# A two-layer convolution and gated feed-forward kernel: the grouped convolution of tiles 6 to 31 as three fp16 products, with its preparation three steps ahead

## The chip, the cores and the metric

The kernel runs on one core of one Trainium2 chip. The metric is the device time of one execution in microseconds (us); the number compared is the median of repeated executions. The engines are PE (TensorE: products, with weight loads shown apart as PEld), DVE (VectorE), ACT (ScalarE), POOL (GpSimd) and SP, which only issues transfers.

## What is computed

The reference, cut to what matters (x is 64 x 64 x 1024; rows are batch times channel):

```python
# layer 0
y   = conv1d(x, weight, pad=4, groups=4, taps=9) + (cond @ c_weight.T)[:, :, None] + fside_bias
x_q = round(y / a_scale).astype(int8)        # a_scale = max|row of y| / 127
w_q = round(weight / w_scale).astype(int8)   # 1024 x 1024
x1  = x + (x_q @ w_q.T * a_scale * w_scale).astype(float16)
# layer 1
x2  = einsum('boi,bih->boh', agg_w, x1) + agg_b      # 64 x 64 matrix per batch
H, z = x2 @ W.T + b, x2 @ A                          # W 1024 x 1024, A 1024 x 32
w   = soft top-2 gate of 8 experts, from H and z at every second row
out = x1 + H + z-delta weighted by the gate          # rank 32
```

## The kernel before

The 4096 rows are 32 tiles of 128 rows (two batches) by 1024. All engines run one program written out by hand, an order for each engine, tied by semaphores. There are three stages: a start (integer weights transposed, small tensors, tiles 0 to 2), a loop `for c in range(3, 32)` that carries layer 0 and the first part of layer 1, and the part behind it, which is nearly all dense product.

**One step c of the loop, on PE:** `conv(c)` (L470), `mix(c - 3)` (x1 times the 64 x 64 matrices, L516), the integer product of tile c - 2 (L532, two halves of eight), cut by three small things: `row_total(c - 3)` (L493), `max_rows(c)` (L539) and `max_back(c)` (L543); then `tokens_out(c - 1)` (transposes, L501) and at odd c `rank_pair(c - 5)` (L569). The convolution works on a layout of x by phases, `x_ph` (128 x 1032 fp32, three buffers), as 16 fp32 products: first 8 for the groups 0 to 3 with 128 rows, then 8 with 64 rows. Each fp32 product shows as two records. Ahead of group 2 it waits for `f_ready`, since groups 2 and 3 use a bank that the integer product of the tile before leaves free only then.

**On DVE:** at even c `rank_out` (L1342, L1343), `conv_bias(c)` (L1283, into `yb`), `row_max(c)` (L1289), `tile_bound` and `tile_scale` (L1319 to L1326, a power of two for x2 of tile c - 3 from its row sums), `layer0(c - 2, 0)` (L1315), `chan_max(c)` (L1294, L1295), `scales(c)` (L1300 to L1306), `layer0(c - 2, 1)`. **On ACT:** `row_sums` (sums of |x1| of a tile, L862), copies of x2 (L879, L882), the integers (L867), `scale_rows` (eight pieces, L889), and W's sums and high halves (L895, L900, L905). **On POOL:** `add_layer0` (x1 = x + f, L1130, two halves), W scaled and its low half (L1135, L1137).

W is used as an fp16 high and low half (`ffn_wT`), and again in the part behind the loop as eight quadrants of sums, prepared in four parts q: `load_t(q)` (SP), `t_scale(q)` (ACT L910), `t_sums(q)` (POOL L1146, four pieces), `t_high(q)` (ACT L921), `t_low(q)` (POOL L1151). Parts q and q + 2 share their stage, so `load_t(2)` waits for the two pieces of `t_low(0)`. Before, `load_t(0)` to `t_low(0)` lie in the last steps of the loop and `t_sums(1)` among the last tiles.

**Behind the loop** PE runs the last mixes and integer products, `dense` (L606) and, between its pieces, the gate: logits (L589), two maxima (L738, L741), then on DVE and ACT a softmax (exponentials on ACT, L1041 and L1043) whose result PE transposes at L746. After it come the pair products (L792) and the rank products (L774). DVE's result `yb` of L1529 is what L746 waits for.

## Time and profile before

| | before |
|---|---|
| median of 3 runs | 651.67 us (650.98 to 651.74) |
| the profiled execution | 651.48 us, of which the span of the trace is 649.7 |
| PE busy | 634.5 us, 98% of the span; 5898 products |
| DVE / ACT / POOL busy | 374.7 / 327.6 / 322.2 us (58 / 50 / 50%) |
| convolution products (L470) | 1024 records, 96.6 us busy, 390 ns mean |
| mean granted clock of PE | 0.995 |
| transfers | 138.37 MB, mean 213 GB/s |

All rows below are of that execution; times in them count from the start of the span, and the rest of its 651.48 us lies outside the span. A bracket at a row's end gives the idle time of the engine ahead of it and what ended it. Of records that follow one another on PE two can be under way at once, so the time that a group takes is read from its start to the start of the next group, not from its length.

### The profile page before, as it was taken

To read this page: it belongs to the slowest core of one execution; us is meant where nothing else is said; L and a number is where in the kernel's file an instruction comes from. 1 tells how busy PE (TensorE), PEld (TensorE's weight loads), DVE (VectorE), ACT (ScalarE), POOL (GpSimd) and SP (SyncE) were. 2 spreads that over 40 slices of the span, in tenths; PEclk is the share of its full clock that TensorE was granted. 3 is DMA by queue.
4 is the path that set the end of the run, shared out by engine and by line. 5 is a ranking of instruction groups with operands and counts; after the bars stand their busy time and mean duration, and the time that the engine had idled before them with its cause. 6 is when DMAs were issued, how large, how long until landed. Compare 5 with 4: busy or idle time off the path is not lost.

```text
span 649.7 us, 14865 instructions
## 1 busy us (share of the span) xinstructions
PE 634.5 (98%) x5898; PEld 336.7 (52%) x5898; DVE 374.7 (58%) x812; ACT 327.6 (50%) x594; POOL 322.2 (50%) x223
## 2 busy tenths in 40 slices
PE   8789999999999999999999999999999999999997
PEld 6545565556555655555554444444444444444443
DVE  5956657665566556667636795745544433444434
ACT  2858898657668766666663335234323223322100
POOL 3012222227778522225475588785766677656400
PEclk9799999999999999999999999999999999999999
DMA  9969877677789798754629114885554444541103
GB/s 311 338 132 368 313 278 294 215 284 257 278 322 338 281 346 289 254 203 148 206 104 333 59 35 152 300 329 194 177 200 139 163 136 157 194 125 71 65 1 129
DMA packets 46705, 138.37 MB, mean 213 GB/s; under 512 B 13180, under 2 KB 13468, under 8 KB 46465
## 3 DMA queue, kind: packets, MB, share of 16 engines
q1 hardware_dynamic: 41886, 120.65, 53.4%
q10 hardware_dynamic: 4752, 16.78, 6.7%
q8 instruction: 47, 0.77, 0.5%
q14 instruction: 20, 0.16, 0.1%
HBM read 89.13 MB, written 48.28 MB: 212 GB/s over the span
## 4 chain that ended last, share of the span: by engine, by line
PE 79%; DVE 1%; issue 0%; ACT 0%; DVEq 0%
PE ps L792 36%; PE ps L532 12%; PE ps L606 9%; PE ps L470 9%; PE ps L516 3%; PE ps L569 3%; PE ps L774 2%; PE ps L501 2%; PE ps L589 1%; PE ps L543 0%; PE ps L539 0%; PE ps L574 0%; DVE unscale L1487 0%; DVE z_lo L1351 0%; DVE ring L1333 0%
## 5 line engine op out<-in xcount | busy, mean ns | idle before, releaser
L1130 POOL TENSOR_TENSOR x<-x_in,f_both 128x512 f32<-128x512 f32 x64 | 74.0, 1157 | 199.0 <-DVE f_both L1315 199.0
L532 PE MATMUL ps<-wqT,yq_both 128*128 128x512 bf16 x512 | 120.5, 379 | 0.8 <-ACT wsc_b L849 0.8
L470 PE MATMUL ps<-x_ph,conv_w 64*64 64x256 f32 (+1 forms) x1024 | 96.6, 390 | 0.0
L889 ACT ACTIVATE yv<-yb,yinv 128x128 f32<-128x128 f32 x256 | 78.0, 390 | 2.3 <-DVE yinv L1306 2.2
L1283 DVE TENSOR_TENSOR yb<-ps,ybias 128x1024 f32<-128x1024 f32 x32 | 39.2, 1224 | 59.5 <-PE ps L470 59.5
L470 PEld LDWEIGHTS ps<-x_ph,conv_w 64*64 64x64 f32 (+1 forms) x1024 | 52.0, 136 | 35.7 <-issue 14.3
L532 PEld LDWEIGHTS ps<-wqT,yq_both 128*128 128x128 bf16 x512 | 45.2, 97 | 48.2 <-issue 0.9
L1166 POOL TENSOR_TENSOR ring<-ring 128x512 f32<-128x512 f32 x52 | 66.0, 1268 | 4.0
L867 ACT ACTIVATE yq_both<-ps 128x1024 bf16<-128x1024 f16 x32 | 32.7, 1022 | 67.2 <-PE ps L501 67.2
L606 PE MATMUL ps<-ffn_wT,ring 128*128 128x512 f16 x288 | 64.6, 379 | 0.0
L927 ACT ACTIVATE ring<-ring,pair_inv 128x1024 f32<-128x1024 f32 x26 | 28.4, 1140 | 54.4 <-DVE x_ph L1583 14.4
L1315 DVE SCALAR_TENSOR_TENSOR f_both<-ps,tok_scale,wsc_b 128x512 f16<-128x512 f32 x64 | 47.8, 748 | 3.6 <-PE ps L532 2.9
L1596 DVE SCALAR_TENSOR_TENSOR x_in<-ps,unscale,x_in 128x512 f32<-128x512 f32 x30 | 22.5, 751 | 43.8 <-PE ps L792 43.8
L606 PEld LDWEIGHTS ps<-ffn_wT,ring 128*128 128x128 f16 x288 | 27.2, 98 | 32.1 <-issue 0.8
L1596 DVE SCALAR_TENSOR_TENSOR wst<-ps,unscale,wst 128x512 f32<-128x512 f32 x28 | 21.0, 750 | 36.0 <-PE ps L792 35.9
L1289 DVE TENSOR_REDUCE rowmax<-yb 128x8 f32<-128x1024 f32 x32 | 39.0, 1220 | 1.0
L516 PEld LDWEIGHTS ps<-mixT,x 64*64 64x64 f32 x2048 | 35.5, 135 | 5.0 <-issue 1.3
L516 PE MATMUL ps<-mixT,x 64*64 64x64 f32 x2048 | 35.6, 218 | 0.0
L1596 DVE SCALAR_TENSOR_TENSOR x<-ps,unscale,x 128x512 f32<-128x512 f32 x21 | 15.8, 751 | 31.5 <-PE ps L792 31.4
L862 ACT ACTIVATE f_both<-x 128x1024 bf16<-128x1024 f32 x32 | 33.4, 1043 | 0.0
L879 ACT ACTIVATE ring<-ps 128x512 f32<-128x512 f32 x52 | 27.8, 585 | 2.6 <-PE ps L516 2.3
L792 PE MATMUL ps<-ffn_wT,x_part 128*128 128x512 f16 x120 | 27.5, 379 | 0.0
(309 smaller groups left out, 1081.9 us busy)
## 6 DMA issues: line engine op xcount, KB each, us to landing
x_ph<-in_x_phases SPq DMA_DIRECT2D x32, 516.0 KB, 6.1
x_in<-in_x SPq DMA_DIRECT2D x32, 512.0 KB, 6.1
x_scratch<-x SPq DMA_DIRECT2D x32, 512.0 KB, 2.9
x_scratch<-ring SPq DMA_DIRECT2D x26, 512.0 KB, 4.3
ring<-x_scratch SPq DMA_DIRECT2D x26, 512.0 KB, 4.4
wst<-in_w_rows SPq DMA_DIRECT2D x12, 512.0 KB, 5.1
x_in<-x_scratch SPq DMA_DIRECT2D x12, 512.0 KB, 4.5
out<-x_in ACTq DMA_DIRECT2D x12, 512.0 KB, 3.4
```

What stands on the lines that cost most here:

```text
L470: return mm(ps_conv[o, g * 2 * MB:(g + 1) * 2 * MB], conv_w[k, g, w.start + o.start:w.start + o.stop], xp[k, g, :, view], start=first, sto ...
L516: last = mm(bank(2 + e)[j * 64:(j + 1) * 64, k * CH:(k + 1) * CH], x1[b, t % 2, l:l + 64], mixT[b, t, b], start=True, stop=True)
L532: last = mm(acc_bank(t, h), yqT[:, t % 2, p, :], wqT[:, p, h * HALF:(h + 1) * HALF], start=p == 0, stop=p == PH - 1)
L606: last = mm(o, x2_cols[:, x2_slot(n), a, k, :], ffn_wT[:, w, k, h * HALF:(h + 1) * HALF], start=k == 0 and i == 0, stop=k == NL - 1 and i ...
L792: last = mm(b, left(a, k), right(w, k), start=fresh and k == 0 and i == 0, stop=k == 3 and i == 2, skip_group_check=True)
L889: last = A(yv[:, s, :], yb[:, t % 2, s, :], ACT.Copy, scale=yinv[:, s:s + 1], bias=MAGIC)
L1130: g.tensor_tensor(x1[:, t % 2, s], x_in[:, t % 3, s], f16[:, s], ALU.add).then_inc(sem("x1_ready"), 1)
L1166: g.tensor_tensor(o, x, y, op).then_inc(sem("s_sum_ready"), 1)
L1283: v.tensor_tensor(yb[:, t % 2, :, :].rearrange("p (b g) m -> p b g m", b=2), ps_conv.rearrange("p (g b m) -> p b g m", g=GRP, b=2), ybias[ ...
L1289: v.tensor_reduce(rowmax[:, :], yb[:, t % 2, :, :], AX.X, ALU.max, apply_absolute_value=True).then_inc(sem("rowmax_ready"), 1)
L1315: v.scalar_tensor_tensor(f16[:, s], acc_bank(t, h), tok_scale[:, t % 4:t % 4 + 1], wsc_b[:, s], ALU.mult, ALU.mult).then_inc(sem("f_ready" ...
L1596: v.scalar_tensor_tensor(buf, src, unscale[:, t:t + 1], buf, ALU.mult, ALU.add).then_inc(sem("pair_folded"), 1)
```

## The change

From tile 6 on (`SPLIT`), the convolution is `split_conv`: x and the weights are each split in an fp16 high and low half, and three products (high-high, low-high, high-low) take the place of one fp32 product: 48 products of 256 columns for a tile. The first six tiles stay as they are. For each such tile x is scaled by a power of two taken from the sum of |x| in its rows, three steps ahead of its use (`LEAD`): ACT `phase_sums(c+3)`, PE `x_total(c+3)`, DVE `phase_bound`, `phase_scale` and `scale_phases(c+3)` (128 x 1032 fp32, L1444), and one step later ACT `phase_high(c+2)` and POOL `phase_low(c+2)` (128 x 1032). `conv_bias` takes the scale back (now with a scalar, L1392).

What is moved for it: the sums of |x1| (`row_sums`) are taken for tiles 0 to 5 only; the bound for x2's scale is made from |x| and the layer's scales in three batches of tiles, in place of one total a step. W's absolute sums go from ACT to DVE (L1469, c = 3 to 10), its scaling from POOL to DVE (`scale_w`, L1474, at c = 13, 15, ..., 27), its sums from ACT to POOL (`w_halves`) and DVE (L1478), one piece of W every second step. `load_phases` runs further ahead, the load for tile 6 ahead of the first load of W. `t_sums(0)`, `t_low(0)` and `t_sums(1)` stand behind the loop, and `load_t(2)` with them.

```diff
-W_ABS, W_BOUND, W_SPLIT, W_SUMS, W_TURN = 3, 11, 13, 19, 27
+W_ABS, W_BOUND, W_SPLIT, W_SUMS, W_TURN = 3, 12, 13, 11, 27
+LEAD = 3
+SPLIT = 3 + LEAD
+BATCHES = ((0, 28), (28, 30), (30, NT))
...
             for c in range(1, NT + 3):
-                if c == NT + 1:
-                    load_t(2)
+                if c >= 3 and c + LEAD + 1 < NT:
+                    load_phases(c + LEAD + 1)
...
+                if c == 2:
+                    load_phases(4)
+                    load_phases(SPLIT)
...
-                if c == W_SPLIT + 9:
+                if c == NT - 2:
                     load_t(0)
                 if c == NT:
                     fetch_x1(0)
                     load_t(1)
+                if c == NT + 2:
+                    load_t(2)
...
+            def split_conv(t):
+                wait(pe, "xl_ready", splits(t))
+                wait(pe, "yb_ready", t)
...
+                parts = ((0, 0), (1, 0), (0, 1))
...
+                for g in range(GRP):
+                    if g == 2:
+                        wait(pe, "f_ready", 2 * t - 4)
+                    for i in range(3):
+                        part(i, g, lo, slice(0, P), slice(P, 2 * P), here, first=g % 2 == 0)
+                        part(i, g, hi, slice(0, P), slice(0, P), there, first=g % 2 == 0)
+                for g in range(2):
+                    for i in range(3):
+                        part(i, g, lo, hi, slice(0, P), there, last=g == 1)
+                        part(i, g + 2, lo, lo, slice(0, P), there, last=g == 1)
+                        part(i, g, hi, lo, slice(P, 2 * P), here, last=g == 1)
+                        last = part(i, g + 2, hi, hi, slice(P, 2 * P), here, last=g == 1)
...
+            def x_total(t):
+                wait(pe, "xsum_ready", splits(t))
+                wait(pe, "yinv_ready", t - LEAD)
+                wait(pe, "x_bound_ready", splits(t - 1))
...
+            def phase_sums(t):
+                act.wait_ge(sem(f"ph_loaded{ph_sem(t)}"), 16 * ph_count(t))
...
+                A(phase_junk, phases(t), ACT.Abs, accum_out=x_sum[:, t:t + 1]).then_inc(sem("xsum_ready"), 1)
...
+            def phase_high(t):
...
+                A(x_split[:, (t - SPLIT) % 2, 0, :], phases(t), ACT.Copy).then_inc(sem("xh_ready"), 1)
...
+            def scale_phases(t):
+                dve.wait_ge(sem("x_scale_ready"), 2 * splits(t))
+                v.tensor_scalar(phases(t), phases(t), x_up[:, t:t + 1], None, ALU.mult).then_inc(sem("xs_ready"), 1)
...
                 layer0(c - 2, 0)
                 chan_max(c)
+                if SPLIT <= c + LEAD < NT:
+                    phase_scale(c + LEAD)
...
                 layer0(c - 2, 1)
                 low(c - 3, 1)
+                if SPLIT <= c + LEAD < NT:
+                    scale_phases(c + LEAD)
...
+                if 0 <= c - W_ABS < NL:
+                    w_abs(c - W_ABS)
+                if c in split_steps:
+                    scale_w(split_steps.index(c))
+                if c - 1 in sum_steps:
+                    w_sums(sum_steps.index(c - 1))
+                if c == 4:
+                    split_weights()
```

The order on DVE, from the second half of `layer0` in step c = 13 to the row maxima of step 14. Before:

```order
L1315 SCALAR_TENSOR_TENSOR f_both<-ps,tok_scale,wsc_b 128x512
L1342 TENSOR_TENSOR z_lo<-ps,zT 40x256
L1343 TENSOR_TENSOR zT<-ps,z_lo 40x256
L1283 TENSOR_TENSOR yb<-ps,ybias 128x1024
L1289 TENSOR_REDUCE rowmax<-yb 128x8
```

And now:

```order
L1430 SCALAR_TENSOR_TENSOR f_all<-ps,tok_scale,wsc_b 128x512
L1444 TENSOR_SCALAR x_ph<-x_ph,x_up 128x1032
L1474 TENSOR_SCALAR wst<-wst,w_up 128x1024
L1495 TENSOR_TENSOR z_lo<-ps,zT 40x256
L1496 TENSOR_TENSOR zT<-ps,z_lo 40x256
L1392 SCALAR_TENSOR_TENSOR yb<-ps,x_down,ybias 128x1024
L1405 TENSOR_REDUCE rowmax<-yb 128x8
```

Two full-width pieces now stand between `layer0` and the next tile's bias.

The order on POOL behind the loop (`wst` is the stage of parts 0 and 2, `row_bias` and `conv_w` that of 1 and 3). Before, from the sums of part 1 on:

```order
L1146 TENSOR_TENSOR row_bias<-row_bias 128x512
L1146 TENSOR_TENSOR row_bias<-conv_w,row_bias 128x512
L1146 TENSOR_TENSOR conv_w<-conv_w,row_bias 128x512
L1146 TENSOR_TENSOR conv_w<-conv_w 128x512
L1130 TENSOR_TENSOR x<-x_in,f_both 128x512 x2
L1146 TENSOR_TENSOR wst<-wst 128x512 x4
L1151 TENSOR_TENSOR wqT<-row_bias,wqT 128x1024
L1151 TENSOR_TENSOR wqT<-conv_w,wqT 128x1024
L1151 TENSOR_TENSOR mixT<-wst,mixT 128x1024 x2
```

And now:

```order
L1224 TENSOR_TENSOR x<-x_in,f_all 128x512 x10
L1245 TENSOR_TENSOR wst<-wst 128x512 x4
L1245 TENSOR_TENSOR row_bias<-row_bias 128x512
L1245 TENSOR_TENSOR row_bias<-conv_w,row_bias 128x512
L1245 TENSOR_TENSOR conv_w<-conv_w,row_bias 128x512
L1245 TENSOR_TENSOR conv_w<-conv_w 128x512
L1250 TENSOR_TENSOR x_ph<-wst,x_ph 128x1024 x2
L1250 TENSOR_TENSOR wqT<-row_bias,wqT 128x1024
L1250 TENSOR_TENSOR wqT<-conv_w,wqT 128x1024
L1245 TENSOR_TENSOR wst<-wst 128x512 x4
L1250 TENSOR_TENSOR mixT<-wst,mixT 128x1024 x2
```

The sums and low halves of part 0 and the sums of part 1 now follow the last tile's addition, where only those of part 2 followed before.

The order on ACT, from the high halves of part 1 to the gate's two exponentials. Now:

```order
L1009 ACTIVATE wqT<-row_bias 128x1024
L1009 ACTIVATE wqT<-conv_w 128x1024
L998 ACTIVATE wst<-wst,w_up 128x1024 x2
L1009 ACTIVATE mixT<-wst 128x1024 x2
L998 ACTIVATE row_bias<-row_bias,w_up 128x1024
L998 ACTIVATE conv_w<-conv_w,w_up 128x1024
L1135 ACTIVATE yb<-yb 128x128
L1137 ACTIVATE yb<-yb 128x128
```

The last six of these stood in the same order before (L910, L921, L910, L910, L1041, L1043), but the scaling of part 2 (`wst`) was then done before the high halves of part 1.

## Rows read from the trace of the kernel before

**Rows 1.** The page, part 4: the chain that ended last, shares of the span.
```profile
PE 79%; DVE 1%; issue 0%; ACT 0%; DVEq 0%
```

**Rows 2.** Timeline of PE, two steps (start, length, engine, line, count).
```profile
203.96 2.93 PE L470 MATMUL ps<-x_ph,conv_w 128*64 128x256 f32 x32
206.71 1.11 PE L516 MATMUL ps<-mixT,x 64*64 64x64 f32 x64
...
212.15 2.98 PE L470 MATMUL ps<-x_ph,conv_w 128*64 128x256 f32 x32
214.95 1.11 PE L516 MATMUL ps<-mixT,x 64*64 64x64 f32 x64
...
220.02 0.22 PE L543 MATMUL ps<-ident,chanmax_rep 8*128 8x8 f32 x1
```

**Rows 3.** Timeline of PE's weight loads, at the second of these convolutions.
```profile
212.98 0.67 PEld L470 LDWEIGHTS ps<-x_ph,conv_w 128*64 128x64 f32 x8 [0.20 <-DVE f_both L1315]
```

**Rows 4.** Timeline of PE, fp16 products of 256 columns (logits and rank products).
```profile
314.57 0.62 PE L577 MATMUL ps<-ring,z_w 128*40 128x256 f16 x8
315.12 2.76 PE L606 MATMUL ps<-ffn_wT,ring 128*128 128x512 f16 x12
```

**Rows 5.** Timeline of DVE, the same two steps.
```profile
202.22 0.75 DVE L1315 SCALAR_TENSOR_TENSOR f_both<-ps,tok_scale,wsc_b 128x512 f16<-128x512 f32 x1
...
204.71 0.42 DVE L1343 TENSOR_TENSOR zT<-ps,z_lo 40x256 f32<-40x256 f32 x1
206.95 1.22 DVE L1283 TENSOR_TENSOR yb<-ps,ybias 128x1024 f32<-128x1024 f32 x1 [1.83 <-PE ps L470]
...
212.17 0.75 DVE L1315 SCALAR_TENSOR_TENSOR f_both<-ps,tok_scale,wsc_b 128x512 f16<-128x512 f32 x1
215.20 1.22 DVE L1283 TENSOR_TENSOR yb<-ps,ybias 128x1024 f32<-128x1024 f32 x1 [2.27 <-PE ps L470]
...
219.36 0.28 DVE L1295 TENSOR_TENSOR chanmax_rep<-ps,chanmax 8x128 f32<-8x128 f32 x1
```

**Rows 6.** Timelines of DVE and of POOL, step c = 8 to 9.
```profile
109.17 2.28 DVE L1277 SCALAR_TENSOR_TENSOR b_parts<-row_bias,s_up,b_parts 32x1024 f16<-32x1024 f32 x1
...
109.22 1.16 POOL L1130 TENSOR_TENSOR x<-x_in,f_both 128x512 f32<-128x512 f32 x1 [1.11 <-DVE f_both L1315]
```

**Rows 7.** Groups of DVE by line and shape.
```profile
L1218 DVE TENSOR_REDUCE wq_max<-ffn_wT 128x1 f32<-128x1024 f32 x8 | 9.6, 1206 | 2.4 <-DMA ffn_wT<-in_w_q 2.4
...
L1231 DVE TENSOR_SCALAR ffn_wT<-ffn_wT,wq_inv 128x1024 f32<-128x1024 f32 x8 | 6.0, 749 | 0.1
```

**Rows 8.** Timelines of ACT and of PE, step c = 3.
```profile
52.27 1.06 ACT L895 ACTIVATE f_both<-wst 128x1024 bf16<-128x1024 f32 x1 [1.07 <-DMA wst<-in_w_nat]
...
51.25 0.18 PE L493 MATMUL ps<-x1sum,ones_b 128*128 128x1 bf16 x1 [0.62 <-ACT f_both L862]
```

**Rows 9.** Timelines of PE and of POOL behind the loop.
```profile
329.86 3.63 PE L532 MATMUL ps<-wqT,yq_both 128*128 128x512 bf16 x16
...
337.19 5.31 POOL L1146 TENSOR_TENSOR wst<-wst 128x512 f32<-128x512 f32 x4
...
346.62 4.22 POOL L1151 TENSOR_TENSOR mixT<-wst,mixT 128x1024 f16<-128x1024 f32 x2
```

**Rows 10.** Timelines of SP's issues and of ACT behind the loop.
```profile
322.43 1.15 SPq L346 DMA_DIRECT2D wst<-in_w_rows  x2
...
328.00 2.19 ACT L910 ACTIVATE wst<-wst,w_up 128x1024 f32<-128x1024 f32 x2 [0.42 <-DMA wst<-in_w_rows]
...
342.71 2.00 ACT L921 ACTIVATE mixT<-wst 128x1024 f16<-128x1024 f32 x2
...
358.63 0.31 ACT L1041 ACTIVATE yb<-yb 128x128 f32<-128x128 f32 x1 [2.28 <-DVE yb L1513]
```

**Rows 11.** Timeline of PE, where the gate's result is wanted.
```profile
364.94 0.27 PE L746 MATMUL ps<-ident,yb 128*128 128x128 f32 x1
```

**Rows 12.** Windows of PE (length, busy, granted clock, DMA share, GB/s).
```profile
26.00:30.00 4.00, 3.16 (x29) 0.50 0.94 294
```

More of the change, by code:

```diff
@@ L216, in pair_banks, with phases, ph_sem, ph_count @@
             return bank(6 + j % 2), bank(0), bank(7 - j % 2)
+        def phases(t):
+            if t == SPLIT:
+                return split_flat[:, PHW:2 * PHW]
+            return x_ph[:, (t if t < SPLIT else t - 1) % 3, :]
+        def ph_sem(t):
+            return 3 if t == SPLIT else (t if t < SPLIT else t - 1) % 3
+        def ph_count(t):
+            return 1 if t == SPLIT else (t if t < SPLIT else t - 1) // 3 + 1
+        def splits(t):
+            return max(t - SPLIT + 1, 0)
+        def batch(t):
+            return [n for n, (lo, hi) in enumerate(BATCHES) if lo <= t < hi][0] + 1
         def x2_slot(n):
@@ L374, in _ @@
             for c in range(1, NT + 3):
-                if c == NT + 1:
-                    load_t(2)
+                if c == 3:
+                    for t in range(5, SPLIT):
+                        load_phases(t)
+                if c >= 3 and c + LEAD + 1 < NT:
+                    load_phases(c + LEAD + 1)
                 if c >= 3:
@@ L460, in agg_weights, with part @@
                             last.then_inc(sem("agg_psum"), 1)
+            def split_conv(t):
+                wait(pe, "xl_ready", splits(t))
+                wait(pe, "yb_ready", t)
+                if t == SPLIT:
+                    pe.wait_ge(sem("conv_h_ready"), 2)
+                xp = x_split[:, (t - SPLIT) % 2, :, :].rearrange("p a (g b m) -> p a g b m", g=GRP, b=2)
+                lo, hi = slice(0, P // 2), slice(P // 2, P)
+                here, there = slice(0, MB), slice(1, MW)
+                parts = ((0, 0), (1, 0), (0, 1))
+                def part(i, g, o, k, w, view, first=False, last=False):
+                    a, n = parts[i]
+                    return mm(ps_conv[o, g * 2 * MB:(g + 1) * 2 * MB], conv_h[k, n, g, w.start + o.start:w.start + o.stop], xp[k, a, g, :, view],
+                              start=first and i == 0, stop=last and i == 2, skip_group_check=True)
+                for g in range(GRP):
[10 more added lines that the diff above has]
+                        last = part(i, g + 2, hi, hi, slice(P, 2 * P), here, last=g == 1)
+                last.then_inc(sem("conv_ready"), 1)
             def conv(t):
@@ L537, in max_rows @@
                 wait(pe, "rowmax_ready", t + 1)
[L538 removed]
+                wait(pe, "x_bound_ready", splits(min(t + LEAD, NT - 1)) if t >= 3 else 0)
+                wait(pe, "bound_ready", len([hi for _, hi in BATCHES if hi <= t]))
                 tr(ps_small[0:8, 0:P], rowmax[:, :], ident[:, :]).then_inc(sem("rowmaxT_ready"), 1)
@@ L686, in _ @@
                 int_product(c - 2, 0, 0, 4)
-                row_total(c - 3)
+                if SPLIT <= c + LEAD < NT:
+                    x_total(c + LEAD)
+                for n in range(2):
+                    if c == BATCHES[n][1]:
+                        batch_total(n)
                 int_product(c - 2, 0, 4, 8)
@@ L720, in _ @@
             int_product(NT - 1, 1)
-            row_total(NT - 2)
             dense(0, 1, 5, 8)
@@ L1174, in _ @@
             for c in range(1, NT + 1):
-                if c == NT - 1:
-                    t_low(0)
+                if SPLIT <= c + LEAD < NT:
+                    phase_low(c + LEAD)
                 add_layer0(c - 1, 0)
                 add_layer0(c - 1, 1)
-                if 0 <= c + 1 - W_SPLIT < NL:
-                    w_low(c + 1 - W_SPLIT)
-                if c == W_SUMS + NL + 1:
-                    t_sums(0)
-                if c == NT - 1:
-                    t_sums(1)
+                if c in split_steps:
+                    w_low(split_steps.index(c))
+                if c + 1 in sum_steps:
+                    w_halves(sum_steps.index(c + 1))
+            t_sums(0)
+            t_sums(1)
+            t_low(0)
+            t_low(1)
             t_sums(2)
-            t_low(1)
             t_low(2)
@@ new lines, in w_abs, with scale_w @@
+            def w_abs(k):
+                dve.wait_ge(sem(f"w_loaded{k % 2}"), 16 * (k // 2 + 1))
+                v.tensor_reduce(w_part[:, k:k + 1], wst[:, k % 2, :], AX.X, ALU.add, apply_absolute_value=True).then_inc(sem("w_abs_ready"), 1)
+            def scale_w(k):
+                dve.wait_ge(sem(f"w_loaded{k % 2}"), 16 * ((NL + k) // 2 + 1))
+                dve.wait_ge(sem("w_scale_ready"), 2)
+                v.tensor_scalar(wst[:, k % 2, :], wst[:, k % 2, :], w_up[:, 0:1], None, ALU.mult).then_inc(sem("w_scaled"), 1)
@@ L1446, in _ @@
                 row_max(c)
-                tile_bound(c - 3)
+                for n in range(2):
+                    if c == BATCHES[n][1]:
+                        dve.wait_ge(sem("total_psum"), n + 1)
+                if SPLIT <= c + LEAD < NT:
+                    phase_bound(c + LEAD)
+                for n in range(2):
+                    if c == BATCHES[n][1]:
+                        batch_bound(n)
                 if c == W_BOUND + 1:
@@ L1457, in _ @@
                 chan_max(c)
+                if SPLIT <= c + LEAD < NT:
+                    phase_scale(c + LEAD)
+                for n in range(2):
+                    if c == BATCHES[n][1]:
+                        batch_scale(n)
                 low(c - 3, 0)
```

335 lines of the change are left out of this document (197 added, 138 removed).

## The prediction

> **What bounds the kernel now.** I read the page's chain first: the work that ended last is PE's for 79% of the span, with next to nothing for any other engine [rows 1]. So a microsecond counts only if PE has less to do, or if PE is made to wait. Then the timeline of PE over two steps of the loop, for what a convolution takes from its start to that of the mix: 203.96 to 206.71 is 2.75 us at even c, behind the rank pair; 212.15 to 214.95 is 2.80 us at odd c [rows 2], of which the weight loads wait 0.20 us for `f_both` of the tile before, until 212.98 [rows 3]. Then DVE's timeline, since the new work sits between `layer0` and `conv_bias`. I call L the end of the second `layer0`: 202.97 and 212.92. The next `conv_bias` starts at 206.95 and 215.20, so DVE is wanted again 3.98 and 2.28 us after L [rows 5]. Last the engines behind the loop, for the four parts of W that are prepared there [rows 9, 10].
>
> **Term 1, the convolution: minus 14.2.** The 32 fp32 records of a tile are 8 pairs and 4 groups of four that run together; 12 times 0.213 us is 2.56, and 2.75 were seen, so 0.19 is start and end. In fp16 a product of 256 columns costs half a record: the fp16 group of [rows 4] runs 8 of them, two at a time, in 0.55 us from start to start, 4 times 0.107 plus 0.12. The change has 12 pairs and 6 groups of four, 18 times 0.107 = 1.92. Behind the rank pair that saves 0.64, 13 times: 8.3. At odd c the second half still can't begin before the wait at 212.98, which doesn't move; behind it stand 8 times 0.213 = 1.70 before and 12 times 0.107 = 1.28 now: 0.43, 13 times: 5.5 (rounded). Row totals that leave the last part of PE's order bring some 0.3. The other end: if every product costs the 0.069 us of [rows 4] (0.55 by 8), and those in fours half of it, a tile takes 24 times 0.069 plus 24 times 0.035 = 2.5 us, and the gain is about 5. I take 14.2, because the fp32 form, with the same shapes, shows only 0.19 us over its columns.
>
> On this the Trainium skill speaks against the change: "TensorE: Matmul & The Clock Gate", Part 3, "The mechanism", says that a weight load overlaps running products only when the row group differs, which the first 24 products, all 128 rows deep, would not meet. By that rule the gain would lie nearer the 5 than the 14.2. The trace does not bear it out for this shape: the 8 products of [rows 4] use all 128 rows and leave 0.12 us in all beside their columns.
>
> **Term 2, the first load: plus 2.2.** The load of x for tile 6 now goes ahead of W's first piece. What stood at that place in the queue landed at 52.27, where ACT waited 1.07 us for it; PE's total of that step ran at 51.25, after a wait of 0.62 [rows 8]. Now `phase_sums(6)` starts at 52.27, takes 1.06 + 0.19, and `x_total(6)` runs at 53.5: 2.2 us later, with the rest of the step behind it in PE's order.
>
> **Term 3, the gate: plus 9.1, and 2 for the clock.** I follow the new orders with the durations of before, at the times of before. The last integer product ends at 333.5 (329.86 + 3.63 [rows 9]); `layer0` and the addition of 0.75 and 1.16 us [rows 5, 6] bring POOL to 335.5. Then `t_sums(0)` 5.31 to 340.8, `t_sums(1)` 5.3 to 346.2, `t_low(0)` 4.22 [rows 9] to 350.4. Only that frees the stage: SP issues `load_t(2)` at 350.5 where it did at 322.43, and the load took 5.5 us (to 328.00 [rows 10]): 356.0. `t_scale(2)` 2.19 to 358.2, `t_sums(2)` 5.31 to 363.5, `t_high(2)` 2.00 to 365.5, `t_scale(3)` 2.2 to 367.7, and only behind these in ACT's queue stands the gate's exponential, which ran at 358.63 [rows 10]. It is 9.1 later. The sum of the gate's steps from there to PE's transpose is as before, and PE had no more than about 0.5 us to spare at 364.94 [rows 11]: it stands idle for 8.6 to 9.1 us (I take 9.1). Queued behind the exponential are the normalised tiles on ACT, the gate's chain on DVE with the folds of the next dense products, and POOL's `t_sums(3)`; so later slack is moved along, not used up. After pauses of PE in the start, its granted clock was 0.50 from 26 to 30 us, with work running [rows 12]: 4 us at half the speed lose 2. Bounds for the term: 0, if PE's order lets it pass the gate (it does not, L746 stands in the middle of `dense`), and 13, if the clock is low twice as long.
>
> **Term 4, DVE late at `conv_bias`: plus 11.8.** `scale_phases` stands right behind L, where POOL's second addition starts. The one place of the trace with a full-width DVE instruction on SBUF operands there is L1277: recorded from 109.17, 0.05 ahead of POOL's addition of 1.16 us, it took 2.28, as though it stood still until POOL's 110.38 and then ran 1.07 [rows 6]. Alone, a multiplication of 128 x 1024 takes 0.75 us, and a reduction 1.21 [rows 7]. If `scale_phases` stands still too, it ends at L + 0.05 + 1.16 + 0.61 (0.75 less the 0.14 of starting, that runs during the wait) = L + 1.82; if not, at L + 0.78.
>
> The need moves forward with the shorter convolution: 3.98 less 0.64 = 3.34 when c is odd (the next step has `rank_out` first), and 2.28 less 0.43 = 1.85 when c is even. Between the next wait of PE on DVE and the end of DVE's work for it lie 0.38 us (219.64 to 220.02 [rows 2, 5]); three small instructions leave that stretch, up to 0.3 more; I take 0.5 as slack.
> - c = 13, 15, ..., 25 (7): `w_halves` on POOL (1.27, a piece of `t_sums`) comes in between, then `scale_w` 0.61: L + 3.65; `rank_out` 0.95 (two of 0.42 and what lies between); 4.6, and the need is 3.34: late by 1.27, PE waits 0.77 each: 5.4.
> - c = 12, 14, ..., 26 (8): half a reduction, 0.6: 2.42 against 1.85, so 0.1 each: 0.8.
> - c = 3 to 10, with `w_abs` of 1.21 each: at odd c 3.03 + 0.95 against 3.34, 0.1 to 0.2; at even c 3.03 against 1.85, 0.6 each; at c = 4 the split of the convolution's weights comes to it (1.9), at c = 9 `delta_weights` (1.5). Together 5.6.
>
> The other instructions (`conv_bias` with a scalar, 0.06 more; `x_total` for `row_total`) cost nothing that I can see. ACT gets two passes of 1.05 a step and gives one, POOL gets 2.1 and gives the scaling of W; both were half idle over the span, and what they prepare is wanted a step later. Ends of the term: 1.3 (the wait is not there; only c = 4 and 9 cost) and 13.5 (slack 0.38).
>
> The page "SBUF — State Buffer" of the Trainium skill, "Who interferes with whom", says that such DVE instructions and GpSimd share a port pair, that whoever issues first has it for the whole instruction, and that reductions never contend. Since DVE is recorded first at L1277 and yet waited, [rows 6] agree on the lock and leave open who gets it; were the rule's "first" DVE here, the term would be 1.3. That is rival B, below.
>
> **The sum**, against the profiled execution: 651.5 - 14.2 + 2.2 + 11.1 + 11.8 = 662.4. The median of the runs shown, 651.67, is 0.2 above it, less than I can forecast: 662.
>
> **The rivals.**
> - A, as above: **662**, and up to 671 with the low end of the convolution's gain. Chance 0.50.
> - B, the other side of the lock: DVE goes first, POOL's addition waits 0.78 (POOL has time). 651.5 - 14.2 + 2.2 + 11.1 + 1.3 = **652**. For it: DVE needs no semaphore there and POOL does. Against it: [rows 6]. 0.22.
> - C, faster: the lateness is covered and the gate's stall is small, because `load_t(2)` or the additions come earlier than I follow them. It decides when `t_scale(3)` ends before 358.6. 651.5 - 14.2 + 2.2 + 1.3 + 1 = **642**. For it: POOL and ACT have half their time free. Against it: the chain of term 3 is a plain sum of durations in a fixed order. 0.16.
> - D, DVE waits as in A, but the gate does not stall: 651.5 - 14.2 + 2.2 + 11.8 = **651**. 0.12.
>
> **How the numbers follow.** A measurement of this kernel can tell about 0.2%, or 1.3 us, from no change. Slower: A, and some of B: 0.67. Same: part of B and of D: 0.13. Faster: C, and part of D: 0.20. The range runs from 645 (between C and D, so that C's 0.16 stays out) to 669 (A with most of the low end): 0.8. A's own range is 655 to 669.
>
> **What would show it.** In the timeline of PE, convolutions of 2.1 us from start to the mix; if 2.5, term 1 is wrong. In DVE's, L1444 with 1.8 us where POOL adds, or 0.75 for B. A wait of PE on DVE near the row maxima of the even steps 14 to 26, 0.8 each. A wait of about 9 us at the gate's transpose (now L836), with a granted clock well below 1 behind it; ACT's row of L1135 right behind L998. A wait of 2 us at `x_total` in step 3. If the loop is no shorter, the time of two of its steps shows which of terms 1 and 4 failed.

## The result

The changed kernel takes 660.81 us (median; 660.11 to 661.34), against 651.5 us for the kernel before on the same chip: a ratio of 1.0143, 95% interval 1.0126 to 1.0161. It is slower by 9.3 us, and the forecast was 662. But the sum came out by terms that erred against each other, as the stages show. The times are those of PE's timelines; stages end where a certain product starts. In the start stage and in step 3 the changed kernel goes from -0.55 to +1.67 against the one before; this part differs from trace to trace (the mix of step 3 starts at 45.57 to 50.52 in all thirteen), so the -0.55 says nothing. The loop from the mix of step 4 to that of step 32 takes 252.21 us in place of 259.52; at the gate PE loses 13.27, and 1.91 behind it.

| stage | before | after | difference |
|---|---|---|---|
| start to the mix of step 3 | 48.56 | 48.01 | -0.55 |
| to the mix of step 4 | 9.74 | 11.96 | +2.22 |
| to the first mix behind the loop (step 32) | 259.52 | 252.21 | -7.31 |
| to the gate's transpose, without its wait | 47.12 | 46.18 | -0.94 |
| wait for the gate | 0 | 13.27 | +13.27 |
| from there to the end of the span | 284.76 | 286.67 | +1.91 |
| span | 649.7 | 658.3 | +8.6 |

The chain of the page, part 4, of the kernel after (compare [rows 1]) has more than PE in it now:

```profile
PE 81%; DMA 5%; DVE 5%; POOL 3%; issue 3%; SPq 2%; ACT 1%; DVEq 0%; POOLq 0%
```

PE's timeline for two steps of the kernel after, the same place as [rows 2], and the weight loads at the second mix (as [rows 3]):

```profile
202.29 2.28 PE L521 MATMUL ps<-x_split,conv_h 128*64 128x256 f16 x48
204.41 1.10 PE L600 MATMUL ps<-mixT,x 64*64 64x64 f32 x64
...
209.84 2.39 PE L521 MATMUL ps<-x_split,conv_h 128*64 128x256 f16 x48
212.27 1.16 PE L600 MATMUL ps<-mixT,x 64*64 64x64 f32 x64
...
212.27 1.02 PEld L600 LDWEIGHTS ps<-mixT,x 64*64 64x64 f32 x64 [0.31 <-POOL x L1224]
```

Behind the rank pair the convolution takes 2.12 us from start to mix (202.29 to 204.41), in place of 2.75; 2.11 was forecast (2.75 less 0.64). In the other step it takes 2.43 in place of 2.80 (209.84 to 212.27), and what ends the last wait is POOL's addition (L1224), not DVE's `layer0`. In the loop PE's loads for the mix waited for this addition 11 times, 3.4 us in all:

```profile
PEld ps L600 <- POOL x L1224: 3.4, 11, 0.3
```

The weight loads of the convolution behind the rank pair are recorded beside its products, which run from 202.29:

```profile
202.08 1.44 PEld L521 LDWEIGHTS ps<-x_split,conv_h 128*64 128x64 f16 x24
...
203.72 0.58 PEld L521 LDWEIGHTS ps<-x_split,conv_h 64*64 64x64 f16 x24 [0.20 <-issue]
```

DVE's and POOL's timelines at that place show why the addition is late:

```profile
200.49 0.74 DVE L1430 SCALAR_TENSOR_TENSOR f_all<-ps,tok_scale,wsc_b 128x512 f16<-128x512 f32 x1
201.15 0.75 DVE L1444 TENSOR_SCALAR x_ph<-x_ph,x_up 128x1032 f32<-128x1032 f32 x1
201.81 1.66 DVE L1474 TENSOR_SCALAR wst<-wst,w_up 128x1024 f32<-128x1024 f32 x1
...
201.31 1.60 POOL L1224 TENSOR_TENSOR x<-x_in,f_all 128x512 f32<-128x512 f32 x1 [1.23 <-DVE f_all L1430]
```

`scale_phases` (L1444) takes 0.75 us: DVE has gone first, and POOL's addition takes 1.60 in place of 1.16 [rows 6]. The second DVE piece, L1474, then stands until POOL is through at 202.91, and takes 1.66, where the last of its eight instances, which started as the addition ended, took 0.74. Over all 26 tiles L1444 never took more than 0.75. So of the two ways in which that place could go, the one of rival B came, at least for the first instruction: DVE goes first.

Behind the loop, ACT's timeline from part 0's high halves to the gate's exponential, that of POOL, SP's issues and PE's wait (as [rows 9 to 11]):

```profile
336.20 2.00 ACT L1009 ACTIVATE x_ph<-wst 128x1024 f16<-128x1024 f32 x2
...
349.74 2.19 ACT L998 ACTIVATE wst<-wst,w_up 128x1024 f32<-128x1024 f32 x2 [7.12 <-DMA wst<-in_w_rows]
357.33 2.00 ACT L1009 ACTIVATE mixT<-wst 128x1024 f16<-128x1024 f32 x2 [5.41 <-POOL wst L1245]
363.64 1.15 ACT L998 ACTIVATE row_bias<-row_bias,w_up 128x1024 f32<-128x1024 f32 x1 [4.31 <-DMA conv_w<-in_w_rows]
...
365.74 0.29 ACT L1135 ACTIVATE yb<-yb 128x128 f32<-128x128 f32 x1
...
340.53 4.21 POOL L1250 TENSOR_TENSOR x_ph<-wst,x_ph 128x1024 f16<-128x1024 f32 x2
...
352.00 5.30 POOL L1245 TENSOR_TENSOR wst<-wst 128x512 f32<-128x512 f32 x4 [3.04 <-ACT wst L998]
...
344.77 0.81 SPq L387 DMA_DIRECT2D wst<-in_w_rows  x2
...
354.25 0.33 SPq L387 DMA_DIRECT2D row_bias<-in_w_rows  x1
...
371.63 0.48 PE L836 MATMUL ps<-ident,yb 128*128 128x128 f32 x1 [13.27 <-DVE yb L1703]
```

The chain is the one of term 3, link by link: `t_low(0)` ends at 344.74, `load_t(2)` goes at 344.77 (forecast 350.5, in a frame that started some 6 us later), `t_sums(2)` at 352.00, `t_high(2)` at 357.33. New is the last link: `load_t(3)` stands in SP's queue behind `load_t(2)`, the row parts (whose own landing SP awaits, to 349.90) and the fetches. It goes at 354.25 and has landed only at 363.64, 9.4 us later, so `t_scale(3)` waits 4.31 us more, and the exponential stands behind it. The granted clock behind the wait, by a window of PE (length, busy, clock, DMA share, GB/s):

```profile
371.63:375.58 3.95, 3.95 (x10) 0.50 0.00 0
```

PE had rested for 13.27 us; it then worked 3.95 us at half the clock (1.2 GHz) and at the full 2.4 GHz behind that. Half of 3.95 is 2.0 us, as much as the 1.91 us of the table.

Step 3, as [rows 8]: the load landed at 52.03 and PE's total waited 3.15 us for the sum over it.

```profile
52.03 1.06 ACT L955 ACTIVATE f_all<-x_split 128x1032 bf16<-128x1032 f32 x1 [2.48 <-DMA x_split<-in_x_phases]
...
53.24 0.18 PE L569 MATMUL ps<-x_sum,ones_b 128*128 128x1 bf16 x1 [3.15 <-ACT f_all L955]
```

### The profile page after: what moved, and what is told of

The parts are those of the page before. It is cut to its first block, busy times and chain, and to the rows that moved or that the text cites. A ratio compares the mean times of both kernels' runs of the same rounds, so it can differ in the third digit from the quotient of the medians.

```text
span 658.3 us, 15754 instructions
## 1 busy us (share of the span) xinstructions
PE 623.8 (95%) x6311; PEld 341.9 (52%) x6311; DVE 423.4 (64%) x858; ACT 337.1 (51%) x591; POOL 377.9 (57%) x249
## 4 chain that ended last, share of the span: by engine, by line
PE 81%; DMA 5%; DVE 5%; POOL 3%; issue 3%; SPq 2%; ACT 1%; DVEq 0%; POOLq 0%
PE ps L882 36%; PE ps L616 15%; PE ps L521 8%; PE ps L691 6%; PE ps L600 4%; PE ps L654 3%; PE ps L864 2%; PE ps L585 2%; PE ps L546 2%; DMA conv_w<-in_w_rows 1%; DMA x_split<-in_x_phases 1%; DMA agg_scratch<-zT 1%; POOL wst L1245 1%; SPq L346 1%; DVE f_all L1430 1%
## 5 line engine op out<-in xcount | busy, mean ns | idle before, releaser
L1224 POOL TENSOR_TENSOR x<-x_in,f_all 128x512 f32<-128x512 f32 x64 | 85.6, 1338 | 117.1 <-DVE f_all L1430 116.7
L1228 POOL TENSOR_TENSOR x_split<-x_ph,x_split 128x1032 f16<-128x1032 f32 x25 | 53.7, 2147 | 32.8 <-ACT x_split L961 29.1
L691 PE MATMUL ps<-ffn_wT,ring 128*128 128x512 f16 x288 | 66.5, 387 | 0.0
L1430 DVE SCALAR_TENSOR_TENSOR f_all<-ps,tok_scale,wsc_b 128x512 f16<-128x512 f32 x64 | 47.7, 745 | 22.6 <-PE ps L616 22.4
L521 PE MATMUL ps<-x_split,conv_h 128*64 128x256 f16 (+1 forms) x1248 | 61.0, 274 | 1.0 <-DVE f_all L1430 0.7
L521 PEld LDWEIGHTS ps<-x_split,conv_h 128*64 128x64 f16 (+1 forms) x1248 | 47.8, 108 | 12.3 <-issue 5.2
L1392 DVE SCALAR_TENSOR_TENSOR yb<-ps,x_down,ybias 128x1024 f32<-128x1024 f32 x26 | 33.4, 1283 | 9.8 <-PE ps L521 9.8
L961 ACT ACTIVATE x_split<-x_ph 128x1032 f16<-128x1032 f32 x25 | 26.5, 1062 | 25.4 <-PE ps L521 25.4
L600 PE MATMUL ps<-mixT,x 64*64 64x64 f32 x2048 | 37.5, 220 | 1.1 <-issue 0.5
L1256 POOL TENSOR_TENSOR yb<-ring,yb 128x512 f16<-128x512 f32 (+1 forms) x8 | 13.0, 1643 | 26.5 <-ACT yb L1028 26.5
```

The lines of the kernel that those rows point to most:

```text
L521: return mm(ps_conv[o, g * 2 * MB:(g + 1) * 2 * MB], conv_h[k, n, g, w.start + o.start:w.start + o.stop], xp[k, a, g, :, view], start=firs ...
L600: last = mm(bank(2 + e)[j * 64:(j + 1) * 64, k * CH:(k + 1) * CH], x1[b, t % 2, l:l + 64], mixT[b, t, b], start=True, stop=True)
L691: last = mm(o, x2_cols[:, x2_slot(n), a, k, :], ffn_wT[:, w, k, h * HALF:(h + 1) * HALF], start=k == 0 and i == 0, stop=k == NL - 1 and i ...
L1224: g.tensor_tensor(x1[:, t % 2, s], x_in[:, t % 3, s], f16[:, s], ALU.add).then_inc(sem("x1_ready"), 1)
L1228: g.tensor_tensor(x_split[:, (t - SPLIT) % 2, 1, :], phases(t), x_split[:, (t - SPLIT) % 2, 0, :], ALU.subtract).then_inc(sem("xl_ready"), 1)
L1430: v.scalar_tensor_tensor(f16[:, s], acc_bank(t, h), tok_scale[:, t:t + 1], wsc_b[:, s], ALU.mult, ALU.mult).then_inc(sem("f_ready"), 1)
```

## The experiments

**The exponentials ahead of `t_scale(3)`.** What holds the gate?

```diff
             t_high(2)
-            t_scale(3)
             act.wait_ge(sem("gate_in_ready"), 1)
             A(gate[:, 3], gate[:, 2], ACT.Exp).then_inc(sem("gate_exp_ready"), 1)
             act.wait_ge(sem("gate_in_ready"), 2)
             A(gate[:, 5], gate[:, 5], ACT.Exp, scale=-2.0).then_inc(sem("gate_exp_ready"), 1)
+            t_scale(3)
```

> The changed kernel with one edit: on ACT the two exponentials of the gate stand ahead of t_scale(3), not behind it. In the trace after, PE waits 13.27 us at the gate's transpose; ACT's t_scale(3) waited until 363.64 for its load and the exponential followed at 365.74, though its input was there at 358.67. Theory (the wait is ACT's queue, the load of part 3 at its head): the exponential starts behind t_high(2), at 359.3, the gate is ready at 365.2, PE waits about 6.9 us, and the time falls by 6.4 us, 7 to 8 if the clock gate gives part of its 1.9 back: 653 to 654.5. Rival (the gate's chain is held on DVE, by its wait for the fetched tile until 354.99 or by instructions that stand still beside POOL): the exponential moves but DVE's steps grow, PE still waits over 11 us, 658 to 661. Rival (t_scale(3), now later, holds part 3 for the pair products): the wait at the gate shrinks and comes back before 400 us.

Measured: 655.26 us, ratio 1.0077 (1.0049 to 1.0106), 4.3 us better than 1.0143 by the ratios. In ACT's timeline the exponential moved to 359.49, right behind `t_high(2)`, and PE waited 7.73 us:

```profile
357.58 2.00 ACT L1009 ACTIVATE mixT<-wst 128x1024 f16<-128x1024 f32 x2 [5.41 <-POOL wst L1245]
359.49 0.29 ACT L1134 ACTIVATE yb<-yb 128x128 f32<-128x128 f32 x1
363.22 0.31 ACT L1136 ACTIVATE yb<-yb 128x128 f32<-128x128 f32 x1 [3.44 <-DVE yb L1695]
...
366.30 0.47 PE L836 MATMUL ps<-ident,yb 128*128 128x128 f32 x1 [7.73 <-DVE yb L1703]
```

So the order on ACT is worth 5.5 us of the wait (13.27 to 7.73). The second exponential came 3.44 us behind the first by DVE's part, where it was 2.51: a little of the rival is there. The exponential's input was there only at 358.93; the rest of the wait lies ahead of that.

**`load_t(2)` behind the fetches.** SP issues `load_t(2)` behind the fetches, and on ACT the exponentials stand ahead of `t_high(2)` too, not only of `t_scale(3)`. SP's part of the edit:

```diff
-                if c == NT + 2:
-                    load_t(2)
...
             for n in range(1, 6):
                 fetch_x1(n)
+            load_t(2)
             load_t(3)
```

> The changed kernel with two edits behind the loop: SP issues load_t(2) behind the five fetches of x1 and the row parts, not ahead of them; on ACT the two exponentials stand ahead of t_high(2) and t_scale(3). Theory: load_t(2) can't go before 344.8 in any case (t_low(0)), but the rows and fetches then go at 330 to 337 and the DVE wait of 5.58 us for the fetched tile is gone; the gate's input is ready at about 353.2, its result at 359 to 361 (POOL's t_sums(2) runs beside it), PE wants it at 358.4 and waits 1 to 3 us. Time 660.8 - 10.5 to 12.5 - 1 to 1.9 of clock: 646.5 to 649.5. Rival (the sums of part 2 and 3 are what counts): the gate is ready but PE waits for them before 400 us; 653 or more.

Measured: 648.25 us, ratio 0.9962 (0.9939 to 0.9984), inside the range given. SP and ACT:

```profile
336.41 1.74 SPq L404 DMA_DIRECT2D x_in<-x_scratch  x3
...
346.34 0.81 SPq L387 DMA_DIRECT2D wst<-in_w_rows  x2
...
353.53 0.31 ACT L1132 ACTIVATE yb<-yb 128x128 f32<-128x128 f32 x1
...
360.35 0.33 PE L835 MATMUL ps<-ident,yb 128*128 128x128 f32 x1 [0.44 <-DVE yb L1702]
```

The fetches go at 336 and not at 351, though `load_t(2)` itself is no earlier (346.34). The gate's result costs PE 0.44 us. So the two queues made the wait: the load of part 2 at the head of SP's queue held the fetches, and ACT's queue held the exponential; no work was saved to remove it. This run changed SP's order and ACT's second place at once; SP's by itself was not run. Its trace says that the step from 7.73 to 0.44 needs both: the exponential's input was there at 353.50, but `t_high(2)` ran from 359.04 to 361.04 here, and an exponential behind it would have come some 7.5 us later. A new wait of 1.5 us shows at PE's product behind the transpose, for ACT.

**One small instruction ahead of `scale_phases`.** Who gets to go first at L (the end of the second `layer0`), and what hangs on it?

```diff
                 dve.wait_ge(sem("x_scale_ready"), 2 * splits(t))
+                link(v.tensor_scalar(probe[:, :], x_down[:, t:t + 1], 1.0, None, ALU.mult))
                 v.tensor_scalar(phases(t), phases(t), x_up[:, t:t + 1], None, ALU.mult).then_inc(sem("xs_ready"), 1)
```

> The changed kernel with one instruction more: a multiplication of 128 x 1 on DVE, waited for, stands between layer0's second half and scale_phases in each step (23 to 26 times). In the trace after, DVE had the scaling of 128 x 1032 done in 0.75 us every time and POOL's addition took 1.60 in place of 1.16. Theory (the one that is there first has both until it is done): DVE now comes 0.15 to 0.25 us late, POOL's addition goes first and takes 1.16, scale_phases takes 1.2 to 1.7 us, conv_bias is late as I had forecast, and the loop is 4 to 9 us longer: 665 to 670. Rival (DVE always wins, or the two only share): scale_phases stays at 0.75 and the time is 661 to 663, 0.1 us a step at most.

Measured: 670.27 us, ratio 1.0308 (1.0266 to 1.0349), 10.7 us slower than the changed kernel by the ratios (1.0308 - 1.0143, by 651). The groups of DVE, with the count and the mean in ns, and the timelines at one step:

```profile
L1446 DVE TENSOR_SCALAR x_ph<-x_ph,x_up 128x1032 f32<-128x1032 f32 x25 | 42.4, 1697 | 0.9
...
209.87 0.14 DVE L1445 TENSOR_SCALAR probe<-x_down 128x1 f32<-128x1 f32 x1
210.05 1.70 DVE L1446 TENSOR_SCALAR x_ph<-x_ph,x_up 128x1032 f32<-128x1032 f32 x1
...
214.32 1.27 DVE L1393 SCALAR_TENSOR_TENSOR yb<-ps,x_down,ybias 128x1024 f32<-128x1024 f32 x1
...
210.03 1.16 POOL L1225 TENSOR_TENSOR x<-x_in,f_all 128x512 f32<-128x512 f32 x1 [1.23 <-DVE f_all L1431]
...
217.06 0.27 PE L625 MATMUL ps<-ident,rowmax 128*8 128x128 f32 x1 [0.33 <-DVE x_bound L1435]
```

An instruction of 0.14 us costs 0.95 for the scaling behind it (1.697 us mean in place of 0.748): POOL is now first with its addition (210.03, 1.16). This is rival A's case, made on purpose, and it lets me check its arithmetic. `conv_bias` starts at 214.32, 1.20 us after the mix that ends the convolution (213.12). A bias that is not late starts 0.24 behind it (206.71 and 206.95, [rows 2, 5]), so this one is late by 0.96 us, where 1.27 was forecast. PE waits 0.33 us at 217.06, not 0.77. So the slack is 0.6 us, near the 0.5 that I took. The loop took 260.92 us, 8.7 more than in the changed kernel, and 7.7 of that lie in two steps: from the mix of step 5 to that of 6 it took 14.43 in place of 9.97, and from step 29 to 30 13.69 in place of 10.42; in the pairs of steps from 18 to 27 it was 0.2 us as a rule. What was heavy there is not the repeated piece but single instructions of a few columns, in `split_weights` and `row_ends_b`, that stood still beside `phase_low` on POOL (2.14 us each):

```profile
74.18 2.03 DVE L1401 TENSOR_SCALAR set_mask_s<-set_mask,s_down 128x8 f32<-128x8 f32 x1
...
294.88 1.99 DVE L1514 SCALAR_TENSOR_TENSOR b_ends<-bias_flat,s_up,b_ends 128x8 f16<-128x8 f32 x1
```

PE then waited 2.76 and 2.45 us for `conv_bias`, and its granted clock fell to half behind each wait (0.57 from 79 to 83 us, 0.50 from 298 to 301), which is 1.5 to 1.7 us more each time. Outside those two steps this order cost about 1 us more than what had happened in the changed kernel.

**Tile 6's load earlier.**

```diff
+            load_phases(SPLIT)
             sp.wait_ge(sem("scratch_saved"), 32)
             sp.wait_ge(sem("mixT_zeroed"), 2)
...
                     load_phases(4)
-                    load_phases(SPLIT)
```

> The changed kernel with one edit: the load of x for tile 6 is issued at about 28 us, where the transfer engines are half idle, in place of 43.23 ahead of W's first piece. Theory: phase_sums(6) no longer waits 2.48 us for it, PE's wait of 3.15 us at x_total in step 3 falls to under 1, and the time falls by 2.2 us (range 1.5 to 3): 658.6. Rival (something else is late next, w_abs on DVE or conv_h's copy on ACT): less than 1 us is gained.

Measured: 656.98 us, ratio 1.0101 (1.0073 to 1.0129), 2.7 us better by the ratios. From the mix of step 3 to that of step 4 it takes 9.41 us in place of 11.96 (before: 9.74). Term 2 is the place of one load in SP's queue, and all of it. (It left at 28.34 us; the DMA share of the changed kernel was 1.04 from 28 to 32 us, not half, but there were 20 us to land in.) In the six traces of kernels that leave this load where it was, that stretch took 11.96 to 15.64 us; in the six with the early load 8.62 to 9.41. The trace of the changed kernel is the mildest of the first six. In the other five PE waited 3.59 to 5.37 us in place of 3.15, and behind that wait its granted clock fell to half for 3.4 us, which it did not in the first: in `e2_load_behind` it was 0.50 from 53 to 56 us.

**Both together.**

> The changed kernel with the edits of e2_load_behind and e4_load6_early together. Theory (the two stalls are independent: one lies in step 3, one behind the loop): against the kernel before the ratio is the product of both gains, 648.3 less 3 = 645 (0.990 to 0.993). Rival (the wait at the load only shifts the loop against the transfers): under 1 us better than e2_load_behind.

Measured: 644.07 us, ratio 0.9894 (0.9869 to 0.9919): the gains of 0.0181 and 0.0042 in the ratio add to 0.992, the measured one is a little better, and the changed kernel without them is faster than the one before.

**`t_low(0)` ahead of `t_sums(1)` on POOL.**

```diff
             t_sums(0)
-            t_sums(1)
             t_low(0)
+            t_sums(1)
             t_low(1)
```

> As e5_both, and on POOL t_low(0) stands ahead of t_sums(1). This frees the stage of part 2 about 3 to 5 us earlier (t_low(0) waits for ACT's high halves at 336 to 338), so load_t(2), its scaling and t_sums(2) come earlier, and ACT is free for the copy behind the gate's transpose, for which PE still waited 1.5 us in e2_load_behind. Theory: 1 to 2 us better than e5_both. Rival: part 1, now later, holds the second tile's products, or POOL's earlier sums make the gate's chain on DVE stand still: no better, or 1 us worse.

Measured: 651.56 us, ratio 1.0018 (1.0003 to 1.0033), 8 us worse than without the swap. I was wrong here; the rival named the cause, but I had put it at 1 us. `load_t(2)` did go some 3 us earlier, but now POOL works without a pause beside the gate's chain on DVE (timelines of both):

```profile
348.70 2.05 DVE L1682 TENSOR_SCALAR yb<-yb,gmx 128x128 f32<-128x128 f32 x1
...
359.25 2.02 DVE L1698 TENSOR_TENSOR yb<-yb 128x128 f32<-128x128 f32 x1
...
361.63 1.66 DVE L1700 TENSOR_SCALAR gsm<-gsm 128x16 f32<-128x16 f32 x1
...
348.54 2.13 POOL L1249 TENSOR_TENSOR wqT<-conv_w,wqT 128x1024 f16<-128x1024 f32 x1
350.62 5.31 POOL L1244 TENSOR_TENSOR wst<-wst 128x512 f32<-128x512 f32 x4
358.99 2.13 POOL L1249 TENSOR_TENSOR mixT<-wst,mixT 128x1024 f16<-128x1024 f32 x1 [3.06 <-ACT mixT L1008]
...
363.96 0.48 PE L835 MATMUL ps<-ident,yb 128*128 128x128 f32 x1 [7.17 <-DVE yb L1702]
```

Instructions of 128 x 128 that take 0.29 us take 2.05, then (L1683, L1684) 1.20 and 1.37, later again 2.02, and one of a few columns (L1700) 1.66 in place of 0.17. In `e5_both` the first of this chain ran at 349.30 to 350.88, in the pause (347.90 to 351.57) in which POOL waited for `t_scale(2)`; the later ones stood beside the sums of part 2 and lost little (at most 0.6 us each). PE waited 7.17 us, and its granted clock was 0.50 for the next 5 us (364 to 369), some 2.5 us more.

**No scaling at all.** What took the 5 to 6 us that the loop didn't gain? This kernel leaves out the scaling of x, so its output lacks that scale.

```diff
-                v.tensor_scalar(phases(t), phases(t), x_up[:, t:t + 1], None, ALU.mult).then_inc(sem("xs_ready"), 1)
+                v.tensor_scalar(probe[:, :], x_down[:, t:t + 1], 1.0, None, ALU.mult).then_inc(sem("xs_ready"), 1)
```

> The changed kernel with the scaling of x's phases (128 x 1032 on DVE) left out: a 128 x 1 instruction stands in its place, so the output lacks that scale. The loop from the mix of step 4 to that of step 32 took 259.5 us before and 252.2 after; the shorter convolutions alone should have given 12.7 to 13.3, 246.5. Theory (DVE's 0.75 and POOL's addition, lengthened by 0.44, cost what is missing: the mixes of odd steps wait for that addition): the loop takes 247 to 249. Rival (the W pieces that were moved to DVE, or the order of the last steps, cost it): the loop stays within 1 us of 252.

Measured, in the trace: the loop took 246.53 us (time 657.44, ratio 1.0104, 1.0076 to 1.0132, with both stalls in it). The first and the last mix of the loop, of the kernel before, the one after and this one:

```profile
58.30 1.11 PE L516 MATMUL ps<-mixT,x 64*64 64x64 f32 x64
...
317.82 1.16 PE L516 MATMUL ps<-mixT,x 64*64 64x64 f32 x64
```

```profile
59.97 1.11 PE L600 MATMUL ps<-mixT,x 64*64 64x64 f32 x64
...
312.18 1.16 PE L600 MATMUL ps<-mixT,x 64*64 64x64 f32 x64
```

```profile
63.23 1.11 PE L601 MATMUL ps<-mixT,x 64*64 64x64 f32 x64
...
309.76 1.16 PE L601 MATMUL ps<-mixT,x 64*64 64x64 f32 x64
```

So the whole change without the scaling gains 13.0 us in the loop (259.52 - 246.53), and the scaling on DVE takes 5.7 of them back (252.21 - 246.53), a little more than the theory had (247 to 249 us for the loop here); the rival is out. The 13.0 are not the convolutions alone. A pair of steps from 18 to 27 falls from 18.52 us to 17.29, by 1.23; over 13 pairs that would be 16.0, by estimate, so the other work that was moved to DVE and POOL takes some 3 us, which no run took apart. The scaling costs without long waits of PE for DVE: 0.07 and 0.21 us in each pair (9.70 and 7.86 us against 9.64 and 7.65 here), and the rest in steps where DVE has single pieces to do besides. The 0.21 is the wait of the mix for POOL's addition: the 11 waits shown above are gone here.

**Two products in place of three.**

```diff
-                              start=first and i == 0, stop=last and i == 2, skip_group_check=True)
+                              start=first and i == 0, stop=last and i == 1, skip_group_check=True)
...
-                    for i in range(3):
+                    for i in range(2):
```

The last two lines stand twice, once for each part of the convolution.

> The changed kernel with two of the three products in each split convolution (the high-low one is left out, so the output is less exact): 32 in place of 48. If PE's columns set the convolution's time, behind the rank pair it shrinks from 2.12 by 6 times 0.107 = 0.64 to 1.48 us, and by up to 0.43 in the other steps. Theory (in the other steps the mix waits for POOL's addition, delayed by DVE's lock): 0.64 in the 13 steps behind a rank pair less what DVE then lacks, and under 0.15 in the others, the loop falls by 4 to 8 us. Rival (weight loads set it): the convolution shrinks by a third of its whole time, 0.7, in both kinds of step, 13 to 17 us.

Measured, in the trace: the loop took 243.79 us (time 654.39, ratio 1.0058, 1.0035 to 1.0081), 8.4 less than with three, just over the 4 to 8 of the theory. The pairs of steps from 18 to 27 took 9.03 and 7.86 us, in place of 9.70 and 7.86. PE's timeline for one pair:

```profile
199.85 1.62 PE L521 MATMUL ps<-x_split,conv_h 128*64 128x256 f16 x32
201.29 1.10 PE L600 MATMUL ps<-mixT,x 64*64 64x64 f32 x64
...
206.73 1.95 PE L521 MATMUL ps<-x_split,conv_h 128*64 128x256 f16 x32
209.16 1.16 PE L600 MATMUL ps<-mixT,x 64*64 64x64 f32 x64 [0.48 <-POOL x L1224]
```

Behind the rank pair the convolution falls to 1.44 us, by 0.68, between the columns' 0.64 and the rival's 0.7. A third of the weight loads went with the products (their time fell from 2.02 to 1.35 us), so this run can't tell the one from the other behind the rank pair. In the other step none of it comes through: the mix waits 0.48 us for POOL's addition. In the changed kernel every second step is already at this limit.

**The scaling on ACT.**

```diff
-                if SPLIT <= c + LEAD < NT:
-                    scale_phases(c + LEAD)
...
             def phase_high(t):
+                act.wait_ge(sem("x_scale_ready"), 2 * splits(t))
+                A(phases(t), phases(t), ACT.Copy, scale=x_up[:, t:t + 1]).then_inc(sem("xs_ready"), 1)
                 act.wait_ge(sem("xs_ready"), splits(t))
```

> As e5_both, with the scaling of x's phases moved from DVE to ACT, one step later, ahead of the high half: 1.14 us more a step on ACT, and nothing between layer0 and conv_bias on DVE but W's pieces. Without any scaling the loop took 246.5 us, with it on DVE 252.2 to 252.5. Theory (DVE's 0.75 and its lock cost 5.7, and ACT, busy about 7.9 us of a step of 8.8, still has room): the loop takes 247 to 249, 3 to 5 us better than the version with it on DVE. Rival (scale_rows, the copies of x2 and the integers come late on ACT): the loop stays at 252 or is longer, PE waits for ACT.

> The same kernel as e5_both, timed on the same chip as e9_scale_on_act for the comparison: 643 to 646, ratio to the kernel before 0.987 to 0.992.

Measured: 645.91 us, ratio 0.9918 (0.9903 to 0.9934), against 644.71, ratio 0.9906 (0.9891 to 0.9922), with the scaling on DVE: no gain. The loop took 252.71 and 251.76 us. From step 12 on it was 176.78 against 180.75, but up to step 12 75.93 against 71.01. The waits of PE (us in total, times, longest) name ACT, in this row and with 1.9 us more for `yq_both`:

```profile
PE ps L584 <- ACT yv L989: 4.6, 5, 1.4
```

**The scaling on ACT from tile 15 on**, on DVE before it (`ACT_FROM = 15` in the conditions of both).

> As e10_both_again, with the scaling of x's phases on DVE for tiles 6 to 14 (steps 3 to 11) and on ACT from tile 15 on. Theory (e9_scale_on_act lost its gain in steps 6 to 10 alone, where ACT also has row sums, the biases of z and the parts of B, and PE waited for it): the loop takes 71.0 us up to step 12 as in e10_both_again and 176.8 from there as in e9_scale_on_act, 247.8 in all, 4 us less than 251.8; time 640 to 642, ratio to the kernel before 0.983 to 0.987. Rival (the late steps gained only because the early ones had let the engines run ahead): the loop is 250 or more.

Measured: 641.77 us, ratio 0.9867 (0.9839 to 0.9896); the loop 248.29 us, where 247.8 was expected. With the early load and the order behind the loop this is the fastest version: 8.8 us under the kernel before, timed beside it, and 18 under the changed one by the ratios (1.0143 - 0.9867, by 651).

## Why the prediction was right, and where not

**The forecast time was right by a balance of errors, and that is luck.** 662 against 660.81; the chance was on slower. Stage by stage, forecast against measured: the loop (terms 1 and 4) -2.4 against -7.3; the load +2.2 against +2.2; the gate with its clock +11.1 against +15.2. The start and the part up to the gate gave 1.5 more that no term had. So the loop came out 5 us better than the sum and the gate 4 us worse.

- **Term 1** was right in its mechanism and somewhat small. The 0.64 of a tile was exact (2.12 us from start to mix). In the other steps 0.37 came of 0.43, held by POOL's addition, which I hadn't among the waits; with the scaling left out that step fell by 0.59 (8.24 to 7.65). The Trainium skill's rule on weight loads ("TensorE: Matmul & The Clock Gate", Part 3, "The mechanism": they overlap running products only when the row group differs) would have put a tile nearer the 2.5 us of the other end. The trace disagrees: the first 24 loads, all 128 rows deep, take 1.44 us beside the products, and the tile takes 2.12.
- **Term 2** was right in its cause, shown by moving the load. That it was right to the tenth is luck: the same order cost 4.3 to 5.9 us in the five other traces that have it (14.08 to 15.64 against 9.74), with a longer wait and a granted clock that fell behind it, which the term didn't have.
- **Term 3** had the right chain and the wrong end. The step that failed is "`t_high(2)` 2.00 to 365.5, `t_scale(3)` 2.2 to 367.7": I took part 3's load as there by then, but it was issued behind the load of part 2, the row parts and the fetches, at 354.25, and took 9.4. I had also followed the new order "at the times of before". The head of the chain came earlier with the loop's gain (`t_low(0)` ends at 344.74, not 350.4) and so did PE, at the gate 6.6 us earlier; the exponential, held by that load, came only 2.0 us earlier (365.74, not 367.7). Of the wait of 13.3 us, 5.5 are shown to be ACT's order by one edit; 7.3 more went when SP's order and a second place in ACT's were changed together. The 2 us for the clock were right (1.9).
- **Term 4** failed in two steps. First, "if `scale_phases` stands still too": it didn't, once in 26 times. Second, what was left out: that DVE, when it goes first, makes POOL's addition late, and that the mix waits for this. Rival B priced that at nothing ("POOL has time"). It had time over the span, but not at that place. So neither A's 11.8 nor B's 1.3: the scaling cost 5.7, by a mechanism of B, and with the 3 us by estimate of the other moved work it is 8.7. Of the 5.7, POOL's delay is seen in 11 steps with about 0.21 each, 2.3 in all; what the rest is made of was not taken apart. Where DVE was made to come second, the lateness was 0.96 and not 1.27, and the slack 0.6, close to the 0.5 taken. One sum of the term is off by a little: 1.82, 1.27 and 0.61 make L + 3.70, not 3.65.
- On the Trainium skill's rule ("SBUF — State Buffer", "Who interferes with whom": whoever issues first holds the shared ports for the whole instruction, the other blocks): the 52 places of two runs agree with it, L1444 at 0.75 with POOL at 1.60, 26 times, and the other way round at 1.70 and 1.16. L1277 [rows 6] is open: it is recorded 0.05 us ahead of POOL and yet stood still. I had weighed that one row above the rule, and took from it who would win.
